# Two linear layers on one core: where the output tiles C begin, and how the first layer's result x1 is added to them

## The reference

```python
def _L0_cond_ref(x, weight, adapter_ids):
    w = weight[adapter_ids]                       # 8 batches, each with its own 2048 x 2048 weight
    return jnp.einsum('bsi,boi->bso', x, w)

def _L1_cond_ref(x, adapter_mapping, W, b, lora_As, lora_Bs):
    base_out = jnp.einsum('bti,oi->bto', x, W) + b
    lora_h = jnp.einsum('bti,bir->btr', x, lora_As[adapter_mapping])
    lora_out = jnp.einsum('btr,bro->bto', lora_h, lora_Bs[adapter_mapping])
    return base_out + lora_out * SCALING          # rank 16, SCALING = 2

x = x + _L0_cond_ref(x, L0_cond_weight, itok_B_3_7)
x = x + _L1_cond_ref(x, itok_B_0_23, L1_cond_W, L1_cond_b, L1_cond_lora_As, L1_cond_lora_Bs)
```

## Time and profile before

| | |
|---|---|
| median of 3 runs | 2561.51 us (2561.50 to 2563.22) |
| the profiled execution | 2564.01 us, its span 2562.3 us |
| PE busy | 2553.4 us of the span |
| DVE busy | 1673.4 us |
| POOL busy | 1251.1 us |
| ACT busy | 876.3 us |
| bytes moved by DMA | 648.03 MB |

### The profile page before, as it was taken

The page is one execution under the profiler, slowest core; times in us unless marked ns, Lnnn a source line. Parts: engine busy times, 40 slices in busy tenths (PEclk is TensorE's granted clock), DMA queues, the critical chain, the costliest instruction groups (busy, mean ns, idle before and its releaser), DMA issues.

```text
span 2562.3 us, 31038 instructions
## 1 busy us (share of the span) xinstructions
PE 2553.4 (100%) x11241; PEld 2111.5 (82%) x11241; DVE 1673.4 (65%) x1889; ACT 876.3 (34%) x1165; POOL 1251.1 (49%) x1471
## 2 busy tenths in 40 slices
PE   9999999999999999999999999999999999999999
PEld 7888888888888888888888888888888888888887
DVE  5445455454354464364443378999998779999995
ACT  4233232232232242242322233343444343333333
POOL 3434434443454343344423466655666665556655
PEclk9999999999999999999999999999999999999999
DMA  8998889998999888899967887457777855446764
GB/s 327 340 297 296 298 284 284 301 285 281 271 296 336 273 285 276 258 293 284 292 193 196 221 310 263 143 173 251 261 246 252 292 168 175 152 151 205 238 224 143
DMA packets 239516, 648.03 MB, mean 253 GB/s; under 512 B 30212, under 2 KB 47108, under 8 KB 239364
## 3 DMA queue, kind: packets, MB, share of 16 engines
q0 software_dynamic: 123440, 393.28, 48.3%
q1 hardware_dynamic: 115636, 252.24, 30.4%
q10 hardware_dynamic: 288, 0.52, 0.1%
HBM read 433.07 MB, written 212.86 MB: 252 GB/s over the span
## 4 chain that ended last, share of the span: by engine, by line
PE 96%; DVE 2%; issue 1%; DMA 0%; SPq 0%; ACT 0%; DVEq 0%
PE bank L948 39%; PE bank L873 18%; PE bank L875 18%; PE bank L874 18%; PE bank L863 1%; PE bank L864 1%; PE bank L963 1%; DVE c L840 1%; DVE xc L774 1%; DVE c L842 0%; DMA x_raw<-xT 0%; DVE xq L764 0%; DVE w_lo L683 0%; DVE xq L760 0%; SPq L316 0%
## 5 line engine op out<-in xcount | busy, mean ns | idle before, releaser
L948 PE MATMUL bank<-xc,wl 128*128 128x512 f32 x4704 | 1088.1, 389 | 0.1
L948 PEld LDWEIGHTS bank<-xc,wl 128*128 128x128 f32 x4704 | 882.6, 188 | 184.5 <-DVE xc L774 0.6
L446 POOL TENSOR_TENSOR wl<-wl 128x512 fp32r<-128x512 f32 x392 | 599.2, 1549 | 408.7 <-ACT wl L614 407.3
L873 PE MATMUL bank<-x_hi,w_hi 128*128 128x512 f32 x2040 | 794.4, 389 | 2.8 <-DVE w_lo L683 2.8
L874 PE MATMUL bank<-x_lo,w_hi 128*128 128x512 f32 x2040 | 794.2, 389 | 0.0
L875 PE MATMUL bank<-x_hi,w_lo 128*128 128x512 f32 x2040 | 794.1, 389 | 0.0
L564 ACT ACTIVATE w_hi<-w_raw 128x1024 fp32r<-128x1024 f32 (+2 forms) x262 | 258.8, 1033 | 975.3 <-PE bank L875 970.5
L795 DVE TENSOR_TENSOR x_raw<-bank,x_raw 128x512 f32<-128x512 f32 x128 | 88.5, 691 | 690.4 <-PE bank L875 640.0
L873 PEld LDWEIGHTS bank<-x_hi,w_hi 128*128 128x128 f32 x2040 | 383.2, 188 | 82.8 <-DVE w_lo L683 3.2
L874 PEld LDWEIGHTS bank<-x_lo,w_hi 128*128 128x128 f32 x2040 | 383.3, 188 | 79.7
L875 PEld LDWEIGHTS bank<-x_hi,w_lo 128*128 128x128 f32 x2040 | 383.3, 188 | 79.7
(11 more groups left out here) (52 smaller groups left out, 1265.4 us busy)
## 6 DMA issues: line engine op xcount, KB each, us to landing
w_raw<-w0T SPq DMA_DIRECT2D x252, 512.0 KB, 7.7
wl<-w1s SPq DMA_DIRECT2D x392, 256.0 KB, 2.8
xss<-x_raw POOLq DMA_DIRECT2D x256, 256.0 KB, 4.5
w1s<-q_raw POOLq DMA_DIRECT2D x196, 256.0 KB, 7.3
q_raw<-w1T POOLq DMA_DIRECT2D x96, 512.0 KB, 9.8
xq<-xss POOLq DMA_DIRECT2D x40, 1024.0 KB, 7.1
x1s<-x_raw POOLq DMA_DIRECT2D x128, 256.0 KB, 2.9
c<-x1s POOLq DMA_DIRECT2D x32, 1024.0 KB, 6.9
```

The costliest lines, as they stand in the source:

```text
L446: pool.tensor_tensor(w[:, 1], w[:, 1].bitcast(F32), w[:, 0].bitcast(F32), ALU.subtract).then_inc(wl_ready, 1)
L873: pe.matmul(sums[s][:], w_hi[s][:, k, :], x_hi[:, k, :], start=(k == 0), stop=False)
L948: mm = pe.matmul(bank[m][:], w[:, w_part, k, :], x[:, x_part, k, :], start=(p == 0 and k == 0 and BEGIN[j]), stop=(p == 2 and k == Q - 1), ...
```

## The change

The copy of x1 in DRAM scratch (`x1s`) is gone. POOL stores x1 in the first stage straight into the output `yT`, and the plain quadrants of x1 that `load_xq` needs are read from there. C no longer begins as x1: the first product that reaches a tile is written to it, and the finished part is added to `yT` by a DMA that accumulates (`store_c`, `accum_op=ALU.add`).

Who writes the first product: in the outer products 1, 2 and 3, where a product reaches two quadrants and begins one of them, ACT copies the bank into the new tile (`begin_c`), right behind its `wl_hi` of the product 4 places later, and DVE only adds it to the other quadrant. In the outer product 0, with one quadrant, DVE writes it with `tensor_copy`. ACT's copy waits for DVE's `acc_free` of that product; DVE, one step later, and PE, before it reuses the bank, wait for ACT's `c_begun`. ACT and DVE also wait until the store of the old content of a part has landed (`y_stored`).

The parts of quadrants 1 and 3 are stored a step later than before, those of 0 and 2 at the same place. A store also waits for the low-rank sums up to that step, and one of quadrant 3 for the load of x1's quadrant 3 out of the same places of `yT`. The order of the low-rank tiles (`LOW_RANK_OF`) is another one, in runs of four in place of eight, so `hm` is loaded 32 times in place of 8, 256 KB each.

For the last part, POOL loads x1 into `xq[3]` four steps before the end, DVE adds it to C in the last step but one (four additions more), and the last part goes out by the same plain stores as before.

```diff
--- before.py
+++ after.py
@@ -64,9 +64,11 @@
-LOW_RANK_OF = [(3, 0), (1, 0), (1, 1), (3, 1), (0, 0), (2, 0), (2, 1), (0, 1)]
+LOW_RANK_OF = [(3, 0, 0), (3, 0, 1), (3, 1, 0), (3, 1, 1), (0, 0, 0), (2, 0, 0), (2, 1, 0), (2, 0, 1),
+               (1, 0, 0), (1, 1, 0), (1, 0, 1), (1, 1, 1), (2, 1, 1), (0, 0, 1), (0, 1, 0), (0, 1, 1)]
...
@@ -121,12 +122,27 @@
         return None if first is None else outer // OUTER * LOW + first
+    def low_rank_until(s):
+        return sum(Q for i in range(s + 1) if low_rank_tile(i) is not None)
+    def begun_by(s):
+        outer, j = divmod(s, INNER)
+        if INNER_FIRST[INNER_INTO[j]] != j or outer % OUTER not in FIRST:
+            return None, None
+        return FIRST.index(outer % OUTER), "DVE" if outer % OUTER == 0 else "ACT"
+    def begun_count(s, m):
+        return sum(Q for i in range(s) if begun_by(i)[1] == "ACT") + (m if begun_by(s)[1] == "ACT" else 0)
...
@@ -296,10 +314,6 @@
             return group * 4 + quad % 2 * 2 + i % 2, quad // 2 * HALF + i // 2 * Q
-        C_LOADS = {4: (3, 3), 7: (3, 1), 11: (3, 2), 14: (0, 0), 16: (0, 3), 19: (0, 1), 22: (0, 2),
-                   25: (1, 0), 28: (1, 2), 31: (1, 1), 34: (1, 3), 37: (2, 0), 40: (2, 2), 43: (2, 1), 46: (2, 3)}
         q_store = [[(0, 0), (6, 1), (5, 3)], [(1, 3), (4, 2)], [(2, 0)], [(3, 1)]]
...
@@ -429,16 +443,17 @@
                 if B_SUM[o] is None:
-                    source = x1s[group * 4 + B_PLAIN[o] % 2 * 2 + right,
+                    source = yT[group * 4 + B_PLAIN[o] % 2 * 2 + right,
                                  B_PLAIN[o] // 2 * HALF + row:B_PLAIN[o] // 2 * HALF + row + Q]
                 else:
                     source = xss[group, B_SUM[o], right, row:row + Q]
                 pool.dma_start(xq[q][:], source.rearrange("t p n -> p t n")).then_inc(xq_loaded[q], 16)
-            def load_c(group, quad, i):
+            def store_c(group, quad, i):
                 b, t = place_of(group, quad, i)
-                pool.dma_start(c_sum[quad][:, i], x1s[b, t:t + Q].rearrange("t p n -> p t n")
-                               ).then_inc(c_loaded[quad][i], 16)
+                pool.dma_start(yT[b, t:t + Q].rearrange("t p n -> p t n"), c_sum[quad][:, i],
+                               accum_op=ALU.add).then_inc(y_stored[quad][i], 16)
             def wl_lo(n):
@@ -458,9 +473,7 @@
                     pool.wait_ge(x1_sum, n + 1)
-                    if n == TILES - 1:
-                        load_c(0, 3, 0)
-                    pool.dma_start(x1s[b, t], x1_raw[s][:]).then_inc(x1_stored[s], 16)
+                    pool.dma_start(yT[b, t], x1_raw[s][:]).then_inc(x1_stored[s], 16)
                     for i in BEGINS[quad]:
@@ -526,27 +539,27 @@
                         pool.wait_ge(x1_stored[i], x1_stores(TILES - 2 + i) * 16)
-                if n in C_LOADS:
-                    load_c(0, *C_LOADS[n])
-                if step == 1 and s >= 1:
-                    for done, load in ((s - 1, False), (s - 3, True)):
-                        if not 0 <= done < SEQ:
+                if step == 2 and s == SEQ - 4:
+                    pool.wait_ge(xc_ready, (SEQ - INNER + 4) * SPLITS)
+                    b, t = place_of(SEQ // PER_GROUP - 1, 0, INNER_INTO[INNER - 1])
+                    pool.dma_start(xq[3][:], yT[b, t:t + Q].rearrange("t p n -> p t n")).then_inc(x1_loaded, 16)
+                if step == 1:
+                    for done in (s - 2, s - 1):
+                        if not 0 <= done < SEQ - 1:
                             continue
                         done_outer, done_j = divmod(done, INNER)
                         group, o = divmod(done_outer, OUTER)
                         i = INNER_INTO[done_j]
                         for quad, _ in INTO[o]:
-                            if LAST[quad] == o and INNER_LAST[i] == done_j:
-                                b, t = place_of(group, quad, i)
-                                if load and group == 0:
-                                    pool.wait_ge(y_stored[quad][i], 16)
-                                    load_c(1, quad, i)
-                                if not load and done < SEQ - 1:
-                                    pool.wait_ge(acc_free, (done + 1) * Q)
-                                    pool.dma_start(yT[b, t:t + Q].rearrange("t p n -> p t n"), c_sum[quad][:, i]
-                                                   ).then_inc(y_stored[quad][i], 16)
+                            if LAST[quad] == o and INNER_LAST[i] == done_j and (quad in (1, 3)) == (done == s - 2):
+                                pool.wait_ge(acc_free, (done + 1) * Q)
+                                pool.wait_ge(low_rank_added, low_rank_until(done))
+                                if quad == 3:
+                                    pool.wait_ge(xq_loaded[i], (group * OUTER + B_PLAIN.index(3) + 1) * 16)
+                                store_c(group, quad, i)
             for quad in range(4):
@@ -659,11 +672,32 @@
                             wl_hi(i)
+            def begin_c(s, m):
+                quad, engine = begun_by(s)
+                if engine != "ACT":
+                    return
+                i, j = INNER_INTO[s % INNER], s % INNER
+                act.wait_ge(acc_free, s * Q + m + 1)
+                if s == INNER and m == 0:
+                    act.wait_ge(h_stored, NB * 16)
+                    act.wait_ge(b_stored, NB * 2 * 16)
+                    for slot in range(2):
+                        act.wait_ge(x1_stored[slot], x1_stores(TILES - 2 + slot) * 16)
+                if s >= PER_GROUP and m == 0:
+                    act.wait_ge(y_stored[quad][i], 16)
+                bank = bank_x if IN_X[j] else bank_y
+                act.activation(c_sum[quad][:, i, m], bank[m][:], ACT.Copy).then_inc(c_begun, 1)
             act.wait_ge(x1_sum, TILES)
             xc_hi(1, 0)
             for n in range(3, SEQ * Q):
                 s, m = divmod(n, Q)
                 wl_hi(n)
+                if n >= Q:
+                    begin_c(s - 1, m)
                 if m >= 2 and s + 1 < SEQ:
@@ -715,11 +749,12 @@
                                          op1=ALU.subtract).then_inc(b_ready, 1)
-            def add_low_rank(i, bank):
+            def add_low_rank(s, i, bank):
                 b, o, quad, inner, m = low_rank_place(i)
                 dve.wait_ge(low_rank_done, i + 1)
-                dve.wait_ge(c_loaded[quad][inner], (i // LOW + 1) * 16)
+                if begun_count(s, 0) > 0:
+                    dve.wait_ge(c_begun, begun_count(s, 0))
                 tile = c_sum[quad][:, inner, m]
@@ -832,18 +867,31 @@
                         dve.wait_ge(acc_free, (s - 1) * Q + m + 1)
+                        if begun_count(s - 1, m + 1) > 0:
+                            dve.wait_ge(c_begun, begun_count(s - 1, m + 1))
+                    if s == SEQ - 1:
+                        dve.wait_ge(x1_added, m + 1)
                     for quad, sign in INTO[o]:
                         tile = c_sum[quad][:, i, m]
-                        if m == 0 and FIRST[quad] == o and INNER_FIRST[i] == j:
-                            dve.wait_ge(c_loaded[quad][i], (group + 1) * 16)
-                        if sign > 0:
+                        if begun_by(s) == (quad, "ACT"):
+                            continue
+                        if begun_by(s) == (quad, "DVE"):
+                            if group > 0 and m == 0:
+                                dve.wait_ge(y_stored[quad][i], 16)
+                            op = dve.tensor_copy(tile, bank[m][:])
+                        elif sign > 0:
                             op = dve.tensor_tensor(tile, bank[m][:], tile, ALU.add)
                         else:
                             op = dve.tensor_tensor(tile, tile, bank[m][:], ALU.subtract)
                     op.then_inc(acc_free, 1)
+                    if s == SEQ - 2:
+                        dve.wait_ge(x1_loaded, 16)
+                        last = c_sum[0][:, INNER_INTO[INNER - 1], m]
+                        dve.tensor_tensor(last, xq[3][:, m], last, ALU.add).then_inc(x1_added, 1)
                     if first_low is not None:
                         dve.wait_ge(acc_free, s * Q + m + 1)
-                        add_low_rank(first_low + m, bank_y[m])
+                        add_low_rank(s, first_low + m, bank_y[m])
                     if s > 0 and m in (0, 1):
@@ -930,6 +978,8 @@
                         pe.wait_ge(acc_free, (s - BANK_BEFORE[j]) * Q + m + 1)
+                        if begun_by(s - BANK_BEFORE[j])[1] == "ACT":
+                            pe.wait_ge(c_begun, begun_count(s - BANK_BEFORE[j], m + 1))
                     if s == 1 and m == 2:
...
```

23 lines of the change are left out of this document (12 added, 11 removed).

## The result

The changed kernel takes 2576.01 us in the median of its runs (2571.92 to 2578.26), the kernel before 2561.6 us beside it: a ratio of 1.0051, interval 1.0040 to 1.0061. It is slower by 14 us. The forecast was 2563.5 us, its range ended at 2571.

The account below looks back on a forecast made before the run. PE was taken as the bound, busy 2553.4 of 2562.3 us. The only term above 0 was 2.0 us where group 0 meets group 1, added to the median of 2561.5: 2563.5 us, range 2560.5 to 2571.

Parts of the forecast that it names:

- the term of 2.0 us more for each store: On the DMA engines, a 1 MB accumulating store takes 5.3 us against 3.3 plain; range 1.7 to 6.8 us more.
- The boundary of the groups: Between group 0 and group 1: the longer store delays the load of xq[0]; without slack PE stops for 2.0 us.
- the entry to outer product 6 of group 1: Quadrant 2's store ahead of xq[0]: 4.3 us of slack hide the 2.0; at the upper bound 2.5 us show.
- The rival of the weight loads: A weight load waits behind a whole accumulating store; one of 7.5 us costs 22 us, 2583 us in all; chance 0.07.
- POOL, 0 us: POOL's issuing: 12 to 48 us more for 31 stores, 25 us less for C loads, no effect on PE.
- DVE, 0 us: DVE loses 96 additions, 65 us, with relief in outer products 1 to 3; PE's gain of 0 to 0.8 taken as 0.
- That hides either: POOL's 407.3 us of waits for ACT, over a microsecond for each product, cover its longer or shorter issuing.
- The thin place of the earlier trace: Group 1's outer product 4: ACT waits 9.39 us for DVE's difference, PE just escapes; expected to stay.
- The end, 0 us: At the kernel's end: the last accumulating store lands at 2559.2, ahead of the end at 2562.3; upper bound 2.9 us late.
- The traffic, 0 us: DMA engines: 106 us of C loads go, 62 us for stores and 20 for hm loads come; no effect on PE.
- the third rival: A weight load waits behind a whole accumulating store: 22 us, or 0 us if queues take turns by packet; chance 0.07.

Follow-up runs that it names:

- e1: The changed kernel with plain stores of the finished C parts in place of accumulating ones, x1 left out of all output parts but the last: 2563.1 us.
- e3: The changed kernel, but DVE writes the first product in outer products 1 to 3 too, in place of ACT's copies; stores still accumulate: 2574.9 us.
- e11: The changed kernel, but DVE's split of xc covers one of its two column blocks from the second stage's third step on: 2568.0 us.
- e7: The changed kernel, but POOL's subtraction for the low part of the weights covers only a quarter of each tile; DMAs the same: 2563.0 us.
- e2: The changed kernel with plain stores, each finished part stored twice by POOL, to the output and to a DRAM scratch: 2567.1 us.
- e6: The changed kernel, but quadrant 2's stores in both groups and quadrant 0's in group 0 come a step later, behind the load of xq[0]: 2575.8 us.
- e12: The changed kernel, whole, but POOL's subtraction for a weight tile is made in two pieces of 256 columns: 2579.2 us.

## Why the prediction was wrong

**The cause was named, its reach was not.** The forecast put the loss on the accumulating store and nothing on ACT's copies, the new waits and the order of the low-rank tiles. e1 shows both, and e3 shows again that ACT's copies cost nothing; the order of the low-rank tiles is cleared by e1 alone, so with plain stores only. But the forecast looked for the loss at places where the chain has no slack, and took the slack elsewhere as safe.

*The engines' work.* Two windows show POOL's queue with stores alone, from 2552 to 2557 us before and from 2563 to 2570 after:

```profile
q0 software_dynamic: 272, 1.05, 51.4%
```

```profile
q0 software_dynamic: 588, 1.17, 92.2%
```

A plain store of 1.05 MB took 0.514 x 5 = 2.6 us of all engines, where the forecast had 3.3. Accumulating, the same bytes took 0.922 x 7 x 1.05 / 1.17 = 5.8 us, where it had 5.3 (6.3 over the whole end). So the term of 2.0 us more for each store was mis-sized: it is 3.2. A packet takes nearly the same time (0.15 us and 0.18 us), but the same bytes go in twice as many. *The landing* is longer than the work: 11.1 us where about 8 were expected, beside the loads around it.

*The boundary of the groups*, 2.0 us, was mis-sized. PE's row there has 61 matmuls in 14.69 us, where 60 took 13.76 and one more 0.23, 13.99 together:

```profile
2005.66 14.69 PE L998 MATMUL bank<-xc,wl 128*128 128x512 f32 x61
```

That is 0.7 us, not 2.0. At the entry to outer product 6 of group 1, where the earlier trace rows showed the slack, `xq[0]` took 12.1 us to land (issued at 2472.9; ACT takes it up at 2485.10), 6 us before, and PE doesn't stop there: what slack there was did hide the store.

```profile
2485.10 1.06 ACT L638 ACTIVATE xc<-xq 128x1024 fp32r<-128x1024 f32 x1 [2.22 <-DMA xq<-xss]
```

*The rival of the weight loads* had the right object and the wrong arithmetic. It asked for a store of over 6.8 us ahead of a load, and gave 0.07. The loads landed after 8 to 11 us with a store of 5.8, as `bm`, `hm` and the load of an `xq` tile add theirs. Its sign, that PE waits at many places after stores, came true. Yet PE waited only 3.2 us for ACT's weights, and e11 shows that even these late tiles would nearly all have been in time.

*POOL, 0 us, and DVE, 0 us,* are **the steps that failed**. "That hides either" was argued from 407 us of waits over 392 products. The mean says nothing of the products behind a late landing, where POOL has no wait at all, works off three or four tiles at 1.3 to 1.8 us and takes DVE with it. The thin place of the earlier trace rows, DVE ahead of ACT, was seen and expected to stay, with the argument that DVE's own work there is unchanged. Its work was; its duration wasn't. The earlier trace rows gave a hint: the subtraction's mean of 1549 ns beside the 1.3 us of those that run alone. In their place the runs showed 10.2 us of PE's time lost to this chain: with POOL short (e7) or DVE relieved (e11) 0 and 1.6 us of missing matmuls are left of 10.7. DVE's busy time fell by 37 us, not 62 to 68; 12 of the difference are the longer split (341.8 us before, 353.9 after), and the rest isn't accounted for. ACT's rose by 48, 55 expected. PE's busy time rose by 4 us, that of held matmuls.

What DVE's split suffers beside POOL is told by its 196 durations: those with no subtraction of POOL beside them take 1.22 us in the mean, and the duration grows by 0.73 us for each us of overlap. POOL pays too: its subtraction takes 1.28 us at best and up to 2.39. DVE's additions out of a PSUM bank take 0.68 us with and without. The clash isn't new, only longer: the longest split took 4.5 us in the kernel before. The Trainium skill, SBUF — State Buffer, section "Who interferes with whom", says that a DVE instruction with two inputs from SBUF contends with a GpSimd instruction that reads SBUF, and that the shared port is an exclusive lock. The trace agrees: 6.67 us are the 1.22 of the split and 5.4 of POOL's 5.54. In this case DVE wasn't let in between any of the four.

*The end, 0 us,* with 2.9 at the upper bound, measured 5.1. It priced the last accumulating store alone, issued 7.0 us before the last matmul. It was issued 6.8 before it, but the one ahead of it, 7.5 us earlier in the kernel before (2544.68 and 2552.18), now was 3.3 us earlier, because late weights had held POOL up ahead of it, and the two queued. e11 and e7 have the same spacing (3.3 and 3.4 us) and a late end without the stall.

*The traffic, 0 us:* right for the outer products 1 to 3, where nothing is lost. In 4 to 6 of group 0 the share of the engines is hardly higher than before (0.82 and 0.80), and 6.3 us are lost all the same. The mean share didn't tell. What e1 leaves as the difference is the form of the stores, each with 5.8 us of engine work in one piece.

The rule cited for the third rival, turns between the queues by the packet (the Trainium skill, DMA: Bandwidth & Descriptors, "Queues, rings and completion order"), is neither borne out nor refuted: POOL's and SP's queues had 526 and 423 packets in the window above, 402 and 497 from 1843 to 1850, and 510 and 816 in that stretch of the kernel before. What was wrong is the step from it to "0 us". A weight load that pays for its own share only can still be late: in the window above SP's queue got a quarter of the engines.

What stays open: why accumulating costs about three times what a second plain store costs (13 against 4 us over e1), when it adds 3.2 us of engine work to a store and the second store 2.6. About 4 us of the difference lie at the end (8.2 against 4.1 us). For the rest the landings, 11.1 us against 9.0 for e2's second store, go the same way, but no run shows why. And e6 and e12, with one profile each, don't tell how much of their stall moved.

No variant beats the kernel before; the nearest, e1 and e7, leave out a part of the computation (x1, and three quarters of the low part of the weights).

## What to carry to other kernels

Slack read from a mean is no slack where work comes in bursts: ask what each engine does right behind the latest landing, and whether two engines that catch up there share a port. An accumulating store has a price in the landing of everything beside it, so count it against the loads that feed the bound engine and against the last store of the kernel, not by its own engine time. Where a stall is chained through several engines, leave out half of one engine's work at a time: that told more here than moving the DMA.

## What the runs showed of the hardware

- An accumulating 1 MB store from SBUF lands after 11.1 us in the median (9.8 at least), a plain one after 5.9 to 6.3 (4.6 at least), and costs POOL 1.31 us to issue in place of 0.77. It takes 5.8 us of all 16 DMA engines in place of 2.6, with twice as many packets for the same bytes.
- DVE's subtraction with both inputs in SBUF (128 x 1024) takes 1.22 us alone and 6.67 beside four of POOL's in a row. Beside POOL's subtractions of 128 x 128, which take 0.67 us in the mean, it is hardly lengthened (1.24, e7).
- POOL's time for a 128 x 512 subtraction in two halves is 2 x 1.0 us, 1.6 in one.
- In one window of 7 us SP's queue, with packets of 0.07 us in the mean, got 26% of the engines beside POOL's with packets of 0.17 us.
